# First attention of a two-layer transformer: two-part fp32r scores in four row tiles, and its layernorm statistics on GpSimd

## The reference

```
x = layernorm(x + attention0(x))     # this case's change lies here
x = layernorm(x + moe(x))
x = layernorm(x + attention1(x))
x = layernorm(x + ffn(x))

def attention0(x):                   # 16 heads of 8 dims, 512 positions, per batch
    q, k, v = split(x @ W_qkv)
    scores = q @ k.T / sqrt(128)     # per head 512 x 512
    return softmax(scores) @ v

def layernorm(x):
    m, v = mean(x), var(x)           # over the 128 numbers of a position
    return (x - m) / sqrt(v + 1e-5)
```

## Time and profile before

| what | value |
| --- | --- |
| median of 3 runs | 1043.92 us (1043.27 to 1044.46) |
| the profiled execution, from first to last instruction (its own time; no other is given for it) | 1041.4 us |
| the first attention in it | to about 406 us |
| a period of its pipeline (147.71 to 191.87) | 44.16 us |
| of it busy: PE, DVE, ACT, POOL | 42.73, 42.55, 34.63, 15.37 us |

### The profile page before, as it was taken

How to read it: one execution, slowest core, us unless ns; L and a number is a source line. 1 busy time by engine, 2 the same in 40 slices (tenths; PEclk the granted TensorE clock), 3 DMA queues, 4 the chain that set the end, 5 groups by cost and what they waited for, 6 DMA issues and landing times. The chain is left out here.

```text
span 1041.4 us, 20120 instructions
## 1 busy us (share of the span) xinstructions
PE 995.5 (96%) x5835; PEld 475.4 (46%) x5835; DVE 834.0 (80%) x1874; ACT 729.9 (70%) x939; POOL 475.6 (46%) x483
## 2 busy tenths in 40 slices
PE   8899999999999999999999999999999999999996
PEld 3222222222222235888888887873332333222485
DVE  6889999999999977787888789897666666643677
ACT  2078777787777786555555555568898888899754
POOL 0332514325053725676777677576442244220275
PEclk9999999999999999999999999999999999999998
DMA  6553222131321003344324323443512331230011
GB/s 198 153 186 119 76 76 89 44 117 46 96 78 52 3 2 101 102 128 145 101 91 156 121 90 117 137 137 102 172 65 61 121 119 63 60 122 1 1 31 52
DMA packets 73981, 97.04 MB, mean 93 GB/s; under 512 B 12669, under 2 KB 42237, under 8 KB 73533
## 3 DMA queue, kind: packets, MB, share of 16 engines
q1 hardware_dynamic: 73928, 96.40, 29.7%
HBM read 68.18 MB, written 27.79 MB: 92 GB/s over the span
## 5 line engine op out<-in xcount | busy, mean ns | idle before, releaser
L741 DVE TENSOR_REDUCE a_nmax<-a_ps_f 128x1 f32<-128x512 f32 x512 | 320.1, 683 | 20.2 <-PE a_ps_f L579 19.7
L497 ACT ACTIVATE a_prob<-a_ps_s 128x1024 f32<-128x1024 f32 x256 | 251.7, 1023 | 77.8 <-PE a_ps_s L646 76.5
L1367 ACT ACTIVATE a_prob<-a_ps_s 128x1024 f32<-128x1024 f32 x256 | 244.4, 1026 | 28.0 <-PE a_ps_s L1419 26.7
L2187 POOL TENSOR_TENSOR moe_hl<-moe_hid,moe_hh 128x512 fp32r<-128x512 f32 x134 | 173.9, 1303 | 84.3 <-ACT moe_hh L2068 84.2
L579 PE MATMUL a_ps_f<-a_ks,a_qs 48*128 48x512 bf16 x512 | 157.9, 386 | 11.8 <-DVE a_nmax L741 4.3
L2058 ACT ACTIVATE moe_ps<-moe_ps 128x512 f32<-128x512 f32 x128 | 74.5, 582 | 111.5 <-PE moe_ps L1981 110.7
L1432 PE MATMUL a_ps_o<-a_prob,a_va 128*32 128x512 f32 x1024 | 136.4, 605 | 1.4 <-DVE a_turned_o L1547 0.5
L659 PE MATMUL a_ps_o<-a_prob,a_va 128*32 128x512 f32 x1024 | 136.4, 605 | 0.5 <-ACT a_prob L497 0.4
L646 PE MATMUL a_ps_s<-a_qs,a_ks 51*128 51x512 bf16 x512 | 132.5, 381 | 1.7 <-ACT a_prob L497 1.5
L579 PEld LDWEIGHTS a_ps_f<-a_ks,a_qs 48*128 48x128 bf16 x512 | 39.7, 93 | 192.2 <-DVE a_nmax L741 162.2
L2109 DVE TENSOR_TENSOR moe_prod<-moe_cw,moe_ps 128x512 f32<-128x512 f32 x128 | 87.2, 681 | 27.4 <-PE moe_ps L1981 26.7
(11 more groups left out here) (302 smaller groups left out, 1640.1 us busy)
## 6 DMA issues: line engine op xcount, KB each, us to landing
moe_cw<-r_weights SPq DMA_DIRECT2D x256, 128.0 KB, 2.9
parts_q<-a_parts SPq DMA_DIRECT2D x48, 256.0 KB, 2.5
parts_k<-a_parts SPq DMA_DIRECT2D x48, 256.0 KB, 2.5
a_qs<-parts_q SPq DMA_DIRECT2D x126, 96.0 KB, 2.4
a_ks<-parts_k SPq DMA_DIRECT2D x126, 96.0 KB, 2.5
a_xt<-in_x_t SPq DMA_DIRECT2D x8, 256.0 KB, 2.8
out_x<-g_X SPq DMA_DIRECT2D x7, 256.0 KB, 2.3
moe_wg<-in_wg SPq DMA_DIRECT2D x1, 1088.0 KB, 6.6
```

Of the source, the lines that this page charges most:

```text
L497: nc.scalar.activation(prob[:, u % PSLOTS, :, :], ps_s[:, u % 2, :, :], ACT.Exp, scale=float(P) ** -0.5).then_inc(exp_done, 1)
L741: nc.vector.tensor_reduce(nmax[:, half_no, h % 2, col:col + 1], ps_f[:, bank, :], AX.X, ALU.max, negate=True).then_inc(max_done, 1)
L1367: nc.scalar.activation(prob[:, u % PSLOTS, :, :], ps_s[:, u % 2, :, :], ACT.Sigmoid, scale=float(HD) ** -0.5).then_inc(exp_done, 1)
L2187: nc.gpsimd.tensor_tensor(hl[:, part_at(j), :], hid[:, hid_at(j), :], hh[:, part_at(j), :], ALU.subtract).then_inc(hl_done, 1)
```

## The change

In the first attention q and k are split into two fp32r parts in place of three bf16 parts, and three pairs of parts are stacked: 3 x 8 = 24 rows for a head (26 in the second pass, with two parts of the maximum). Four heads lie in four row tiles of 32 in place of two in tiles of 64. The order of the heads in the first pass becomes four heads in turn, shifted by two against the second pass. The splitting takes two POOL instructions for q, for k and for a half of the maxima, in place of four. SP writes with two DMAs in place of three, reads with four DMAs of 24 rows in place of two of 48, and moves a half of the maxima with four DMAs in place of two. The maxima are turned in float32, 128 columns at once. The rows of ones are set by POOL at the start, the selection matrix is float32 and copied by POOL, and the first four heads are placed by four matmuls in place of twelve. For batches 0 to 6 DVE no longer takes the statistics; POOL sums by seven halvings, takes the mean, subtracts it, squares, sums by seven halvings again, and normalises (`normalise`). What else is in the pipeline, its turns and its banks stay as they are.

```diff
@@ sizes
-MXR = QKR + PARTS
+LEVELS = 7
+NORM_STEPS = 2 * LEVELS + 4
+TERMS = 3
+QTR = P // HG
+FQKR = TERMS * HD
+FMXR = FQKR + 2
+PLACED_ROWS = P - QTR + FQKR
...
+def sum_columns(pool, ops, src, half, to, step, at):
+
+    width = src.shape[2] // 2
+    ops.tensor_tensor(half[:, :, 0:width], src[:, :, 0:width], src[:, :, width:2 * width], ALU.add).then_inc(step, 1)
+    for k in range(1, LEVELS):
+        width //= 2
+        dst = half[:, :, 0:width] if width > 1 else to.unsqueeze(2)
+        pool.wait_ge(step, at + k)
+        ops.tensor_tensor(dst, half[:, :, 0:width], half[:, :, width:2 * width], ALU.add).then_inc(step, 1)
...
 def s1_place(n):
 
-    return 2 * (n // (2 * NT)) + n % 2, n // 2 % NT
+    return HG * (n // (HG * NT)) + (n + 2) % HG, n // HG % NT
...
+def quarter_rows(tile, h, n_rows):
+
+    return tile[QTR * (h % HG):QTR * (h % HG) + n_rows, h // HG, :]
...
+def read_terms(sp, scratch, dst, grp, done):
+
+    for i in range(HG):
+        src = bass.AP(tensor=scratch.tensor, offset=(i * NG + grp) * T, ap=[[H * T, FQKR], [1, T]])
+        sp.dma_start(dst[QTR * i:QTR * i + FQKR, grp, :].bitcast(F32), src).then_inc(done, 16)
+
+
+def split_in_two(eng, ops, src, parts, k, split, parts_done, zero):
+
+    ops.tensor_tensor(parts[:, 0, :], src, zero, ALU.add).then_inc(split, 1)
+    eng.wait_ge(split, k + 1)
+    ops.tensor_tensor(parts[:, 1, :], src, parts[:, 0, :], ALU.subtract).then_inc(parts_done, 1)
...
@@ sync
             def first_stacks():
 
+                sp.wait_ge(filled, 2)
                 for n in range(2):
-                    sp.wait_ge(first_mid, 2 * n + 2)
-                    write_first_pairs(sp, scratch[n][0], parts, n, first_out[n])
+                    sp.wait_ge(first_high, 2 * n + 2)
                     sp.wait_ge(first_low, 2 * n + 2)
-                    write_last_pairs(sp, scratch[n][0], parts, n, first_out[n])
-                for grp in range(PLACED * 2 // HG, NG):
+                    write_terms(sp, scratch[n][0], parts[n], n, first_out[n])
+                for grp in range(1, NG):
...
@@ tensor
             def turn_max(b, half_no):
 
                 pe.wait_ge(mt_parts, 2 * b + half_no + 1 + MP_C)
-                nc.tensor.transpose(turned_max(half_no), msplit[:, :, :, :], identb[:, :]).then_inc(mt_done, 1)
+                nc.tensor.transpose(turned_max(half_no), msplit[:, :, :, :, :], ident[:, :]).then_inc(mt_done, 1)
...
-                nc.tensor.matmul(ps_f[:, bank, :], stack_rows(qs[p], h, QKR)[:, qt * P:(qt + 1) * P],
-                                 stack_rows(ks[p], h, QKR), start=True, stop=True).then_inc(s1_done, 1)
+                nc.tensor.matmul(ps_f[:, bank, :], quarter_rows(qs[p], h, FQKR)[:, qt * P:(qt + 1) * P],
+                                 quarter_rows(ks[p], h, FQKR), start=True, stop=True).then_inc(s1_done, 1)
...
-                    mm = nc.tensor.matmul(ps_s[:, u % 2, i, :], stack_rows(ks[p], h, MXR)[:, kt * P:(kt + 1) * P],
-                                          stack_rows(qs[p], h, MXR), start=True, stop=True)
+                    mm = nc.tensor.matmul(ps_s[:, u % 2, i, :], quarter_rows(ks[p], h, FMXR)[:, kt * P:(kt + 1) * P],
+                                          quarter_rows(qs[p], h, FMXR), start=True, stop=True)
...
@@ vector
-                            if tail and t == STATS_AT:
-                                stats(b - 1)
...
@@ gpsimd
+            for i in range(2):
+                nc.gpsimd.memset(ks[i][:, :, :].bitcast(F32), 1.0).then_inc(filled, 1)
...
+            def normalise(b):
...
+                sum_columns(pool, nc.gpsimd, att, half_sums, sums[:, :], norm_step, at)
+                pool.wait_ge(norm_step, at + LEVELS)
+                nc.gpsimd.tensor_tensor(mean, sums[:, :], share[:, :], ALU.mult).then_inc(norm_step, 1)
...
                 if u0 == 0 and tail:
                     add_x(b - 1)
-                    layernorm_pool(nc, pool, g, ln, b - 1)
-                    layernorm_apply_pool(nc, pool, g, ln, b - 1, att, pool_gate)
+                    normalise(b - 1)
```

More of the change, by code:

```diff
@@ L53 @@
 WARM = (5, 2, 3)
-PLACED = 2
 RC, CW_EARLY = 8, 3
@@ L307, in attention0 @@
     X, ident = g["X"], g["ident"]
-    scratch = [[nc.dram_tensor(f"parts_{n}{i}", [PAIRS, P, T], BF16).ap() for i in range(2)] for n in "qk"]
+    scratch = [[nc.dram_tensor(f"parts_{n}{i}", [TERMS, P, T], F32).ap() for i in range(2)] for n in "qk"]
     with ExitStack() as ctx:
@@ L350, in attention0 @@
         first_out = [sem(f"first_out{n}") for n in "qk"]
-        first_done, first_high, first_rest, first_mid, first_low = (
-            sem("first_" + n) for n in ("done", "high", "rest", "mid", "low"))
-        select_in, placed = sem("select_in"), [sem(f"placed{j}") for j in range(PLACED)]
+        first_done, first_high, first_low = (sem("first_" + n) for n in ("done", "high", "low"))
+        select_in, sel_done, placed, filled = sem("select_in"), sem("sel_done"), sem("placed"), sem("filled")
         s1_done, max_done = sem("s1_done"), sem("max_done")
@@ L522, in _ @@
                     act.wait_ge(first_done, 2 * n + i + 1)
[L523 to L532, removed]
+                    nc.scalar.activation(parts[n][:, 0, in_half(i)], ps_s[:, n, i, 0:T // 2], ACT.Copy).then_inc(first_high, 1)
+            act.wait_ge(filled, 2)
+            act.wait_ge(first_done, 4 + 1)
+            nc.scalar.activation(qs[0][0:PLACED_ROWS, 0, :], ps_s[0:PLACED_ROWS, 0, 0, :], ACT.Copy).then_inc(placed, 1)
             act.wait_ge(cleared, 5)
@@ L825, in split_qk @@
                 pool.wait_ge((q_taken, k_taken)[n], b + 1)
-                split_in_parts(pool, nc.gpsimd, qk[:, n, :], rest[:, n, :], parts[:, n, :, :], 2 * b + n, split,
-                               parts_done, g["zero"][:, :].broadcast_to([P, T]))
+                split_in_two(pool, nc.gpsimd, qk[:, n, :], parts[n][:, :, :], 2 * b + n, split, parts_done,
+                             g["zero"][:, :].broadcast_to([P, T]))
             def units(b, p, u0, u1, qk_on, fore, back, tail):
@@ L2521, in layouts @@
     r["w_qkv"] = np.ascontiguousarray(np.concatenate([w[:, :P][:, order], w[:, P:2 * P][:, order], w[:, 2 * P:]], 1))
-    select = np.zeros((P, 2, PARTS, PLACED, HALF + QKR), dtype=np.float32)
-    for n, pairs in enumerate(((0, 1, 0, 1, 0, 2), (1, 1, 2, 2, 0, 2))):
-        for j in range(PLACED):
-            for half in range(2):
-                for r_at, part in enumerate(pairs):
-                    for d in range(HD):
-                        select[d * H + half * HH + j, n, part, j, HALF * half + r_at * HD + d] = 1.0
-    r["select"] = select.reshape(P, -1).astype("bfloat16")
+    select = np.zeros((P, 2, 2, PLACED_ROWS), dtype=np.float32)
+    for n, parts in enumerate(((0, 0, 1), (0, 1, 0))):
+        for j in range(HG):
+            for r_at, part in enumerate(parts):
+                for d in range(HD):
+                    select[d * H + j * NG, n, part, QTR * j + r_at * HD + d] = 1.0
+    r["select"] = select.reshape(P, -1)
+    heads = at % HH * 2 + at // HH
     r["gate_t"] = np.ascontiguousarray(np.asarray(i["L0_ffn_gate_weight"]).T)
```

174 lines of the change are left out of this document (102 added, 72 removed).

## The result

The changed kernel takes 1272.37 us (median of 4 runs, 1261.43 to 1276.31) against 1043.77, a ratio of 1.2168 with a 95% interval of 1.2104 to 1.2233. The forecast was 1070.5 with 1080 as its upper end: the sign was right, the size was not. The profiled execution took 1276.31 us, its span is 1274.4.

The account below looks back on a forecast made before the run. A loop through both DVE and PE bounds the kernel, 2.48 us per group of four scores. Loads 21.9, turned maxima 0.8, last period 1.9 and start 2 add 26.6 to the 1041.4 span: 1068.0, plus 2.5 gives 1070.5; range 1051 to 1080.

Parts of the forecast that it names:

- the part on the start: Start of the kernel: later loads make PE stand 0 to 5 us once, taken as 2; any clock effect within that bound.
- fp32r scores in small tiles stream more slowly: Rival for the scores: slower streaming, or a start costing over 6 us, gives over 1077 us; chance 0.07.
- The loop and its loads: First attention's groups of four: two exposed fp32r weight loads add 0.196 us a group, 112 times, 21.9 us (0 to 25.3).
- the maxima turned in float32: Float32 turns ahead of a fourth score, twice a batch: 14 x 0.06 = 0.8 us slower (0.4 to 1.8).
- The statistics: Layernorm statistics taken from DVE, 1.20 us a period, hide behind the v product: gain 0 (at most 8.4 us).
- GpSimd: POOL takes over the layernorm sums, about 7 us a batch by size, fits its idle time: cost 0.
- no change: Whole kernel: a difference within 0.2%, 2 us, cannot be told from the time before; chance 0.03.
- The start and the last period: One PE wait at the start, 2 us (0 to 5); exposed second-pass loads in the last period, 1.9 (0 to 3.1).
- I take 0: Start: split maxima come -1.8 to +2.3 us later, taken as 0, so DVE's wait of 2.40 us stays.
- the stand of batch 2's q product: Early periods: SP issues batch 2's x later, so PE waits for it 0 to 5 us once, taken as 2.
- Rival 1: First attention's groups: four tiles take PE out of the loop, DVE alone sets the pace, 1025 us; chance 0.10.
- Rivals 2 and 3: Score loads: only one stays exposed, 1060 us, chance 0.14; or loads cost nothing, 1042 to 1049, chance 0.05.

Follow-up runs that it names:

- rows_56: Changed kernel, still fp32r, each score contracted over 56 rows in a tile of 64 instead of 24 in 32, two heads added, loads of ones omitted: 1070.98 us.
- s1_bf16: Changed kernel with only the first-pass scores reading the upper 16 bits as bf16, second-pass scores fp32r; its measured time is not in the text.
- ln_only: Kernel before with only the layernorm's mean and variance of batches 0 to 6 moved to GpSimd, scores still bf16 with 48 rows: 1045.75 us, ratio 1.0023.
- scores_only: Changed kernel with the layernorm's mean and variance back on VectorE, scores as changed: 1263.27 us.
- bf16_four: Changed kernel with both passes' scores reading the upper 16 bits as bf16, 24 and 26 rows in four tiles; its measured time is not in the text.
- dummy: Changed kernel with one more 128x128 bf16 matmul of 512 columns ahead of every fourth first-pass score: 1344.48 us.

## Why the prediction was wrong

**The step that failed** is the sentence in the part on the start: a stand of PE "lies in a stretch whose granted clock is 0.91 [...] so a little more may follow; it is within the bound". It took a fall of the clock to last as long as with 48-row bf16 scores (3.41 us, the 0.91 of the earlier trace rows), and every duration of the loop from rows at 1.00: that the change could move the clock itself stands in the sum at nothing, without a reason. With the changed scores the clock does not come back while the first attention runs: 563 us at 0.50, and 1274.4 - 1069.1 = 205 us between the changed kernel and rows_56, whose clock stays up. No rival had this; the upper end of 1080 allowed for "fp32r scores in small tiles stream more slowly", which at 1.00 they do not (0.49 to 0.50 with the exposed load).

**The loop and its loads: near at full clock.** The sum ran against the span 1041.4 and gave 1068.0; rows_56 has 1069.1. Its six later periods, from the split at 107.81 to that at 394.67, take 47.81 each, where 47.4 was forecast and 44.14 was before. Two more lines, of s1_bf16 (windows, one period) and of ln_only (the same), divide the rise:

```profile
138.37:182.97 44.60, 42.45 (x279) 14.17 (x279) 41.54 (x71) 34.80 (x40) 16.49 (x31) 1.00 0.25 79
```

```profile
148.48:192.66 44.18, 42.86 (x280) 11.64 (x279) 41.55 (x71) 34.63 (x40) 21.55 (x40) 1.00 0.26 78
```

With bf16 scores in the first pass alone the period is 44.60: fp32r there costs 47.75 - 44.60 = 3.15 us, and 16 x 0.196 = 3.14 was the term for its loads. The two runs also differ in rows and tiles (56 in 64 against 24 in 32), so that the close agreement may be luck; scores_only's group of the changed scores gives 2.70 - 2.48 = 0.22 against 0.196. What no row showed then, a load of few rows, is shown now: at 1.00 the first-pass load reads 181 ns with 24 rows (the changed kernel, 20 to 40 us) and 183 with 56 (rows_56), against 93 in bf16, so that fewer rows saved nothing. The 0.44 that is left over 44.16 was forecast as 0.1, for the maxima turned in float32; what makes the rest was not tried apart.

**The statistics: right.** In ln_only DVE is busy 41.55 in a period in place of 42.55, 1.00 less where 1.2 was forecast, and the period is 44.18 in place of 44.16.

**GpSimd: right to 0.23%.** It is busy 21.55 in place of 15.37 in ln_only, and 16.6 with the shorter splits in rows_56 (1.2 more, where about 3 was forecast). The one wait for it in a period of ln_only, 0.8 us of PE's weight load for the split maxima, is as long in the kernel before. ln_only's 0.23%, 2.4 us, is clear of noise and just outside what was called no change; its profiled execution has 6.8 us at 0.50 near 41 us, against 3.41 before, and the remainder is not assigned.

**The start and the last period: within their bounds.** SP's and POOL's timelines of the changed kernel answer to the earlier trace rows:

```profile
18.83 1.59 SPq L308 DMA_DIRECT2D a_qs<-parts_q  x4
...
22.09 2.57 SPq L460 DMA_DIRECT2D a_ks<-a_ks  x4
25.20 0.85 SPq L502 DMA_DIRECT2D g_X<-in_x  x1
```

```profile
36.25 1.04 POOL L313 TENSOR_TENSOR a_parts<-a_qk,g_zero 128x512 fp32r<-128x512 f32 x1 [29.77 <-DMA g_X<-in_x]
```

A read takes 0.40, within 0.29 to 0.46; the four loads of ones take 2.57, where about 1 was forecast. POOL begins 5.0 us later than before, has four split instructions less, and DVE's reduction behind the maxima is at 42.41 in place of 42.33: "I take 0" held. PE's timeline of rows_56 has the stand of batch 2's q product that was priced at 2:

```profile
72.24 1.13 PE L615 MATMUL a_ps_f<-a_xt,a_w 128*128 128x512 f32 x2 [2.17 <-DMA a_xt<-in_x_t]
```

Its second split of batch 0 is at 57.85, 1.6 us before that of the kernel before, the first period is 5.86 longer (3.67 and the 2.17), six periods 22.0, and the rest of the span 1.4 (1.9 was forecast for the last period): -1.6 + 5.9 + 22.0 + 1.4 = 27.7, the whole difference of the spans. That the forecast of 26.6 came so near is in part luck: the seven periods took 25.7 more where 22.7 was forecast (loads and turned maxima), the start and the last period 2.0 where 3.9 was, and rows_56 has no loads of ones at the start.

**Rival 1** (four tiles take PE out of the loop) is refuted where the clock was up: bf16_four, with bf16 loads and four tiles, has a period of 44.54 (splits at 254.30 and 298.84), no shorter than 44.16. **Rivals 2 and 3** fall with the 0.22 a group and the 3.15 a period; one load would have given half of either.

Open stays why a score over few rows counts so, why fp32r counts more than bf16, and why a full-array matmul in each group changed nothing. That the clock makes the 205 us is shown; what in a score of few rows keeps it down is not. The rows show that it is so, and for each size only in one profiled execution.

## What to carry to other kernels

A duration read from a trace holds for the granted clock of its row. Before matmuls are made to use fewer rows of the array, look where the clock falls in the trace of before, how long it stays down and what brings it back: if the new work is thinner, price the whole stage at half rate as a case of its own, with a chance. When the time of a TensorE kernel moves much more than the sum of its terms, read the granted clock by windows before any engine's busy time: a busy share of 95% says nothing of the rate.

## What was not expected of the hardware

TensorE ran at 1.2 GHz for 563 us while the profile has it busy 95% of the time, and for 614 us at 99.8% in dummy. And one loop ran at both levels: that of bf16_four spent 106 us at 0.50 and then 65 us at 1.00, with the same order of matmuls in its periods.
